# DLRM tower on one core: the first two one-hot fields taken as a couple, a third place for half grams, and another order of tile 3's rows and the dense parts

## What is computed

```python
e = jnp.stack([tbl_0[ids[:, 0]], ..., tbl_25[ids[:, 25]]], axis=1)
T = jnp.concatenate([r_dense[:, None, :], e], axis=1)
Z = jnp.einsum('bnd,bmd->bnm', T, T)
z = Z[:, iu0, iu1]                      # pairs n < m
h = jnp.concatenate([z, r_dense], axis=1)
h = jnp.maximum(h @ W_top1 + b_top1, 0.0)   # 479 -> 512
h = jnp.maximum(h @ W_top2 + b_top2, 0.0)   # 512 -> 256
y = h @ W_top3                              # 256 -> 1
```

## Time and profile before

| what | value |
|---|---|
| times of the kernel before | 118.52, 598.5, 118.72 us; median 118.72 |
| profiled execution | 118.53 us, its span 116.7 us |
| TensorE busy (matmuls, 1008) | 108.4 us, 93% of the span |
| VectorE busy | 85.6 us, 73% |
| ScalarE busy | 80.9 us, 69% |
| GpSimd busy | 65.3 us, 56% |
| one-hot matmuls, lines 473 and 475 | 128 each, 51.8 and 50.2 us busy |
| gram matmuls, line 431 | 512, 15.1 us busy |

### The profile page before, as it was taken

The page is one execution under the profiler, slowest core; times in us unless marked ns, Lnnn a source line. Parts: engine busy times, 40 slices in busy tenths (PEclk is TensorE's granted clock), DMA queues, the critical chain, the costliest instruction groups (busy, mean ns, idle before and its releaser), DMA issues.

```text
span 116.7 us, 2626 instructions
## 1 busy us (share of the span) xinstructions
PE 108.4 (93%) x1008; PEld 91.0 (78%) x1008; DVE 85.6 (73%) x179; ACT 80.9 (69%) x151; POOL 65.3 (56%) x66
## 2 busy tenths in 40 slices
PE   4889799899999999999999999989699998998993
PEld 4757478588688887887888788978599987898990
DVE  5699999889597789969778751499996841567131
ACT  4469990994999999999997794499993602455011
POOL 7387787788777877877787775003063720004000
PEclk9999999999999999999999999999999999999999
DMA  3799749999999529992111112001011110001000
GB/s 74 262 361 406 275 105 411 382 398 363 400 316 380 218 71 367 405 338 65 45 45 32 35 45 60 13 0 26 6 23 51 34 32 6 0 3 21 6 3 1
DMA packets 7751, 17.75 MB, mean 152 GB/s; under 512 B 2078, under 2 KB 3002, under 8 KB 7610
## 3 DMA queue, kind: packets, MB, share of 16 engines
q1 hardware_dynamic: 5770, 14.13, 33.1%
q0 software_dynamic: 1824, 3.25, 9.7%
q10 hardware_dynamic: 144, 0.20, 0.6%
HBM read 17.33 MB, written 0.00 MB: 148 GB/s over the span
## 4 chain that ended last, share of the span: by engine, by line
PE 66%; ACT 11%; DMA 8%; DVE 8%; issue 4%; SPq 1%; ACTq 0%; DVEq 0%
PE work L473 20%; PE work L475 19%; DMA table<-small 8%; PE work L431 8%; PE work L421 6%; PE work L532 5%; ACT Zt L574 4%; PE tp L457 4%; DVE hot L739 3%; PE work L415 3%; ACT t_hi L594 2%; ACT table L566 2%; DVE Zt L574 2%; ACT hot L623 2%; DVE t_lo L708 2%
## 5 line engine op out<-in xcount | busy, mean ns | idle before, releaser
L403 POOL DMA_INDIRECT rows<-tbl,idx x48 | 58.4, 1217 | 18.3 <-issue 13.3
L473 PE MATMUL work<-hot,t_hi 128*128 128x512 f32 x128 | 51.8, 405 | 2.2 <-DVE hot L739 1.1
L475 PE MATMUL work<-hot,t_lo 128*128 128x512 f32 x128 | 50.2, 392 | 0.0
L739 DVE TENSOR_SCALAR hot<-ids_bc,rownum 128x1024 fp32r<-128x1024 int32 (+1 forms) x59 | 38.9, 699 | 7.2 <-PE work L475 7.1
L473 PEld LDWEIGHTS work<-hot,t_hi 128*128 128x128 f32 x128 | 24.0, 188 | 10.8 <-DVE hot L739 2.9
L475 PEld LDWEIGHTS work<-hot,t_lo 128*128 128x128 f32 x128 | 24.1, 188 | 4.4
L594 ACT CAST t_hi<-table 128x1280 fp32r<-128x1280 f32 (+3 forms) x16 | 16.8, 1050 | 5.8 <-DMA table<-small 5.5
L708 DVE TENSOR_TENSOR t_lo<-table,t_hi 128x1280 fp32r<-128x1280 f32 (+3 forms) x16 | 19.5, 1217 | 1.2 <-ACT t_hi L594 1.0
L431 PE MATMUL work<-XT 128*58 128x52 f32 x512 | 15.1, 217 | 2.4 <-ACT Zt L574 1.1
L431 PEld LDWEIGHTS work<-XT 128*58 128x58 f32 x512 | 14.3, 133 | 3.7 <-issue 2.4
L328 POOL DMA_DIRECT2D Zt<-table x9 | 4.7, 531 | 22.1 <-DVE table L566 22.1
(11 more groups left out here) (47 smaller groups left out, 58.1 us busy)
## 6 DMA issues: line engine op xcount, KB each, us to landing
table<-small SPq DMA_DIRECT2D x8, 640.0 KB, 7.9
ids_bc<-ids_oh SPq DMA_DIRECT2D x6, 512.0 KB, 6.1
table<-small SPq DMA_DIRECT2D x4, 512.0 KB, 7.6
w_sb<-w SPq DMA_DIRECT2D x1, 1024.0 KB, 7.7
rows<-tbl,idx POOLq DMA_INDIRECT x48, 4.1
table<-small SPq DMA_DIRECT2D x2, 320.0 KB, 5.0
ids_bc<-ids_oh SPq DMA_DIRECT2D x2, 256.0 KB, 4.5
w_sb<-w SPq DMA_DIRECT2D x1, 512.0 KB, 8.8
```

What stands on the lines that cost most here:

```text
L403: nc.gpsimd.indirect_dma_start(rows[:, t, place - FIRST, :], None, tbls[f], bass.IndirectOffsetOnAxis(ap=idx[:, t, place - FIRST:place - F ...
L473: nc.tensor.matmul(bank, t_hi[:, i % PARTS, c * D:(c + 1) * D], hot[:, k % HOTS, :], start=row_chunk(i, c) == 0, stop=False)
L475: last = nc.tensor.matmul(bank, t_lo[:, i % PARTS, c * D:(c + 1) * D], hot[:, k % HOTS, :], start=False, stop=row_chunk(i, c) == n - 1)
L739: nc.vector.tensor_scalar(hot[:, k % HOTS:k % HOTS + n, :], ids_bc[:, ids_slot(f):ids_slot(f) + n, :], rownum[:, v, at:at + 1], None, ALU. ...
```

## The change

- `SINGLES` goes: fields 0 and 1 are a couple like the others. Only the first chunk of each (`LONE` = 2 chunks) has a one-hot of its own, of width 512; their ids come as two loads, those of field 1 now second in SyncE's queue. ScalarE makes the last couple of chunks of tables 0 and 1.
- Only table 0 comes in parts, of four and four chunks (`HEADED` = 1, `HEAD` = 4, before two tables in three and five); table 1 comes whole. `LOW_PARTS` and ScalarE's first steps follow.
- Ids go to slot f % 6, and the wait for a free slot begins with field 6.
- All eight PSUM banks are one tensor, and `HOMES` gives the place of each half: 0 and 1 as before, and the two `tp` banks for the third half (`IN_TP`). A half waits for the drain of the last half in its own place. The third half waits for the row copies before it; rows (3,1) and (3,2) wait until the third half is drained.
- In the order of steps, rows (3,0) go right behind the look-ups (copied by VectorE), (3,1) behind layer 1 of tile 0 (copied by ScalarE); the dense part of tile 0 goes behind the fourth half, that of tile 2 ahead of the seventh.
- VectorE makes `h1` of tile 2 ahead of its last high copy of the eighth half instead of behind it.

```diff
-VECTOR_ROWS = [(3, 1)]
+VECTOR_ROWS = [(3, 0)]
-HEADED = 2
-HEAD = 3
+HEADED = 1
+HEAD = 4
-SINGLES = 2
+LONE = 2
-ACT_EVERY = 5
-ACT_TABLES = [3, 5, 6, 7, 8, 9, 10, 11, 12, 13]
+ACT_TABLES = [0, 1, 3, 5, 6, 7, 8, 9, 10, 11, 12, 13]
+BANKS = 8
+IN_TP = 3
+HOMES = [0, 1, IN_TP, 0, 1, 0, 1, 0]
-LOW_PARTS = {(i, 5 if i < SINGLES else 4 if OH_CHUNKS[i] == 8 else 6): (i + 1, 0, OH_CHUNKS[i + 1])
-             for i in range(1, K_OH - 1)}
-LOW_PARTS.update({(0, 0): (0, 0, HEAD), (0, 4): (0, HEAD, OH_CHUNKS[0]), (0, 5): (1, 0, HEAD),
-                  (1, 1): (1, HEAD, OH_CHUNKS[1])})
+LOW_PARTS = {(i, 4 if OH_CHUNKS[i] == 8 else 6): (i + 1, 0, OH_CHUNKS[i + 1]) for i in range(K_OH - 1)}
+LOW_PARTS.update({(0, 0): (0, 0, HEAD), (0, HEAD): (0, HEAD, OH_CHUNKS[0]), (0, 6): (1, 0, OH_CHUNKS[1])})
...
-    steps += [("dense", 0, 0), ("burst", 0, 0), ("gram", 0, 0), ("burst", 0, 1), ("gram", 0, 1), ("rows", 3, 0),
-              ("burst", 1, 0), ("gram", 1, 0), ("rows", 3, 1), ("burst", 1, 1), ("gram", 1, 1), ("burst", 2, 0),
-              ("gram", 2, 0), ("layer1", 0, 0), ("layer1", 0, 1), ("burst", 2, 1), ("gram", 2, 1), ("dense", 1, 0),
-              ("layer2", 0, 0), ("layer1", 1, 0), ("layer1", 1, 1), ("rows", 3, 2), ("burst", 3, 0), ("gram", 3, 0),
-              ("dense", 2, 0), ("layer2", 1, 0), ("burst", 3, 1), ("gram", 3, 1), ("layer1", 2, 0), ("layer1", 2, 1),
+    steps += [("rows", 3, 0), ("burst", 0, 0), ("gram", 0, 0), ("burst", 0, 1), ("gram", 0, 1), ("burst", 1, 0),
+              ("gram", 1, 0), ("burst", 1, 1), ("gram", 1, 1), ("dense", 0, 0), ("burst", 2, 0), ("gram", 2, 0),
+              ("layer1", 0, 0), ("layer1", 0, 1), ("rows", 3, 1), ("burst", 2, 1), ("gram", 2, 1), ("dense", 1, 0),
+              ("layer2", 0, 0), ("layer1", 1, 0), ("layer1", 1, 1), ("rows", 3, 2), ("dense", 2, 0), ("burst", 3, 0),
+              ("gram", 3, 0), ("layer2", 1, 0), ("burst", 3, 1), ("gram", 3, 1), ("layer1", 2, 0), ("layer1", 2, 1),
...
+def halves_before(n):
+
+    return max([m + 1 for m in range(n) if HOMES[m] == HOMES[n]], default=0)
...
 def ids_slot(f):

-    return f if f < SINGLES else (f - SINGLES + IDS - 2) % IDS
+    return f % IDS
...
-                n = 1 if i < SINGLES else 2
-                if i >= SINGLES + 2:
-                    sp.wait_ge(hot_used, groups_used(first_hot(ids_free(i))))
-                sp.dma_start(ids_bc[:, ids_slot(i):ids_slot(i) + n, :],
-                             ids_oh[i:i + n, :, :].rearrange("f p b -> p f b")).then_inc(ids_in[i], 16)
+                if i >= IDS:
+                    sp.wait_ge(hot_used, groups_used(first_hot(i - IDS + 2)))
+                sp.dma_start(ids_bc[:, ids_slot(i):ids_slot(i) + 2, :],
+                             ids_oh[i:i + 2, :, :].rearrange("f p b -> p f b")).then_inc(ids_in[i], 16)
...
-            table_ids(0)
+            for f in range(LONE):
+                sp.dma_start(ids_bc[:, f, :], ids_oh[f, :, :]).then_inc(ids_in[f], 16)
...
+                    if IN_TP in HOMES[:halves]:
+                        pe.wait_ge(gram_dve, HOMES.index(IN_TP) + 1)
+                        pe.wait_ge(gram_act, HOMES.index(IN_TP) + 1)
...
-                    if halves >= HALVES:
-                        pe.wait_ge(gram_dve, halves - HALVES + 1)
-                        pe.wait_ge(gram_act, halves - HALVES + 1)
-                    couples(t, i, halves % HALVES, 0, QH // 2).then_inc(burst_done, 1)
+                    if HOMES[halves] == IN_TP:
+                        rows_moved(banks)
+                    if halves_before(halves):
+                        pe.wait_ge(gram_dve, halves_before(halves))
+                        pe.wait_ge(gram_act, halves_before(halves))
+                    couples(t, i, HOMES[halves], 0, QH // 2).then_inc(burst_done, 1)
...
             high_part(0, 0, HEAD)
             distance(0)
             high_part(0, HEAD, OH_CHUNKS[0])
-            one_hot(mine_in(0)[0])
-            high_part(1, 0, HEAD)
-            distance(1)
-            high_part(1, HEAD, OH_CHUNKS[1])
+            high_part(1, 0, OH_CHUNKS[1])
             for kind, t, i in STEPS:
                 if kind == "onehot":
-                    rest = mine_in(i)[1:]
-                    if rest and i < HEADED:
-                        one_hot(rest[0])
-                    if i + 1 < SINGLES:
-                        one_hot(mine_in(i + 1)[0])
-                    if i + 2 < K_OH:
+                    if 1 < i < K_OH - 2:
                         high_part(i + 2, 0, OH_CHUNKS[i + 2])
-                    if i >= SINGLES:
-                        for m in mine_in(i):
-                            one_hot(m)
-                    if 0 < i <= SINGLES:
-                        copy_lookups(i - 1)
-                    elif i > SINGLES + 1:
+                    for m in mine_in(i):
+                        one_hot(m)
+                        if i == 0:
+                            distance(1)
+                    if i <= 1:
+                        high_part(i + 2, 0, OH_CHUNKS[i + 2])
+                    if i > 1:
                         copy_lookups(i - 2)
...
+            def units_done(t):
+
+                if t >= 2:
+                    dve.wait_ge(l2_full, t - 1)
+                dve.wait_ge(l1_part, 2 * (t + 1))
+                nc.vector.tensor_scalar(h1[:, t % 2, :, :], l1[:], 0.0, None, ALU.max).then_inc(h1_ready, 1)
...
-                    copy_high(nc.vector.tensor_copy, t, i, halves % HALVES, first)
+                    copy_high(nc.vector.tensor_copy, t, i, HOMES[halves], first)
+                    if t == TILES - 1 and i == 1:
+                        units_done(t - 1)
                     if t < TILES - 1 or i == 1:
-                        copy_high(nc.vector.tensor_copy, t, i, halves % HALVES, second).then_inc(gram_dve, 1)
+                        copy_high(nc.vector.tensor_copy, t, i, HOMES[halves], second).then_inc(gram_dve, 1)
```

More of the change, by code:

```diff
@@ L265, in dlrm_tower @@
         h1 = apart[:, :, 0:H1].rearrange("p t (u b) -> p t u b", b=P)
-        tp = pb("tp", [P, 2, BATCH])
-        work = pb("work", [P, LOOKUP_BANKS, BANK])
-        gr = work[:, 0:GRAM_BANKS, :].rearrange("p (h k) (q n) -> p h (k q) n", h=HALVES, n=COUPLE * PAD)
+        banks_all = pb("banks_all", [P, BANKS, BANK])
+        tp = banks_all[:, LOOKUP_BANKS:BANKS, :]
+        work = banks_all[:, 0:LOOKUP_BANKS, :]
+        gr = banks_all.rearrange("p (h k) (q n) -> p h (k q) n", k=HALVES, n=COUPLE * PAD)
         l2 = work[:, GRAM_BANKS, :]
@@ L307, in l1_block @@
                 return tp[:, u, 0:P]
-            return work[:, u - COUPLE, 0:P]
+            return work[:, u, 0:P]
         def l2_block(t, v):
@@ L313, in l2_block @@
                 return l2[:, 0:H2] if t < TILES - 2 else work[:, GRAM_BANKS + 1, 0:H2]
-            return work[:, GRAM_BANKS - 1 - v, 0:P]
+            return work[:, 1 - v, 0:P]
         l3 = tp[0:1, 0, P:2 * P]
@@ L607, in distance @@
                 act.wait_ge(ids_in[f], 16)
+                if f == 0:
+                    act.wait_ge(ids_in[1], 16)
                 act.wait_ge(rownum_ready, 2)
@@ L671, in _ @@
                     first, second = range(SAMPLES - ACT_SAMPLES, SAMPLES)
-                    copy_low(nc.scalar.copy, t, i, halves % HALVES, first)
-                    copy_low(nc.scalar.copy, t, i, halves % HALVES, second).then_inc(low_act, 1)
+                    copy_low(nc.scalar.copy, t, i, HOMES[halves], first)
+                    copy_low(nc.scalar.copy, t, i, HOMES[halves], second).then_inc(low_act, 1)
                     if t == TILES - 1 and i == 1:
-                        copy_high(nc.scalar.copy, t, 0, (halves - 1) % HALVES, second).then_inc(gram_act, 1)
-                    copy_high(nc.scalar.copy, t, i, halves % HALVES, first)
+                        copy_high(nc.scalar.copy, t, 0, HOMES[halves - 1], second).then_inc(gram_act, 1)
+                    copy_high(nc.scalar.copy, t, i, HOMES[halves], first)
                     if t < TILES - 1 or i == 1:
-                        copy_high(nc.scalar.copy, t, i, halves % HALVES, second).then_inc(gram_act, 1)
+                        copy_high(nc.scalar.copy, t, i, HOMES[halves], second).then_inc(gram_act, 1)
                     halves += 1
@@ L729, in _ @@
                     dve.wait_ge(ids_in[f], 16)
-                    n = 1 if i < SINGLES else 2
-                    for c in range(0, OH_CHUNKS[i], n):
+                    for c in range(OH_CHUNKS[i]):
                         if (i, c) in LOW_PARTS and i + c:
@@ L833 @@
     for i, n in enumerate(OH_CHUNKS):
-        if i < SINGLES:
-            table = chunks[i]
-        else:
-            f = pair_of(i)
-            part = slice((i - f) * n // 2, (i - f + 1) * n // 2)
-            table = np.stack([chunks[f][:, part], chunks[f + 1][:, part]], axis=2)
+        f = pair_of(i)
+        part = slice((i - f) * n // 2, (i - f + 1) * n // 2)
+        table = np.stack([chunks[f][:, part], chunks[f + 1][:, part]], axis=2)
```

49 lines of the change are left out of this document (23 added, 26 removed).

## The result

| | before | changed kernel |
|---|---|---|
| median | 119.12 us (118.3 to 598.5, 20 runs) | 118.05 us (117.05 to 118.94, 20 runs) |
| ratio to before | | 0.991, 95% interval 0.989 to 0.994 |
| profiled execution, span | 118.53, 116.7 us | 118.94, 117.1 us |

The change takes 1.1 us off. Over 20 runs the kernel before is at 119.12, so 0.4 of the distance from 116.3 to 118.05 is the starting point and the rest a gain of 1.1 in place of 2.4. A ratio here compares only runs within 1.5% of the fastest of their kernel, while a median is over all runs.

What follows compares the result with a forecast made beforehand. It took TensorE to bound the look-ups, with time lost to stops in the start and tail. Profiled 118.53 - 2.5 (tail) + 0.2 (front) = 116.2, or 116.3 us against the median of 118.72; range 115.1 to 117.8.

Steps and rivals of the forecast that it cites:

- The couple makes chunk 16 1.3 us later: Start: wider distance, cast and one-hot in ScalarE's chain move chunk 16 from 15.21 to 16.5, 1.3 us later.
- The 1.1 us of stops behind it go: Chunk 16 to first transposes: ids 4 and 5 with own slots let table 5 come early, removing 1.1 us of stops.
- What is late next: nothing until chunk 46: Look-ups after the start: no new wait until chunk 46, which waits about 0.3 us for ScalarE as before.
- the front's sum: Start up to the first transposes: +1.3 - 1.1 = +0.2 us, with bounds of -0.6 and +1.8.
- Tail -2.5: End of look-ups to layer 1 of tile 3: stops of 3.1 us become 0.6, so it starts at 107.0, not 109.53.
- the low moves of tile 0, issued until 81.7 and 0.4 earlier in the new order (layer 1 asks for them at 83.3): Tail, before layer 1 of tile 0: a cover with no room, costing its own lateness, 0.5 us at most.
- Start ahead: Rival, start: table 1 lands by 7.9, chunk 16 at 15.8, front -0.5, time 115.6 us; chance 0.14.
- Table 1 at 10.2: Rival, start: table 1 lands 7.6 us after issue, the chain moves 1.6 us, time 117.9 us; chance 0.12.
- The third place only moves the wait: Rival, tail: drains become the bound, at 2.75 us each dense 1 waits 1 us, time 117.3 us; chance 0.17.
- Slower by a late table: Rival, start: each microsecond table 1 lands after 8.55 costs one; slower from 13.4, time 121.2 us; chance 0.04.

Runs made afterwards that it cites:

- the new start alone: Kernel before with only fields 0 and 1 as a couple, the id slots and the matching SyncE, ScalarE and VectorE orders, old tail: 1.010 to before.
- the trace with freed slots: Kernel before with only ids of field f in slot f mod 6, so ids 4 and 5 load at once: 1.014 to before.
- the repeated run: The changed kernel timed and traced once more with no edit: 0.993 to before.
- the three traces named under the table: Clock fell to 0.50 for 3 to 4 us: changed, held to chunk 15 (0.995); changed, tables 0 and 1 pairs on VectorE (0.997); slots freed, new tail (0.994).

## Why the prediction was off, step by step

**"The couple makes chunk 16 1.3 us later": right.** It comes at 16.81 in the profiled run (forecast 16.5). By the table's start column, single fields with freed slots have their first transposes at 26.76 (mean of six), the couple at 27.80 (mean of seven, without the two rows at a lower clock in the start): +1.0.

**"The 1.1 us of stops behind it go": right as far as it went.** Single fields with the queue as before or held to chunk 15 have 28.00 (mean of five), with the freed one 26.76: -1.2. The sum of both, -0.2 for the start (forecast +0.2), is the same within the scatter of single traces, 27.4 to 28.8 for one and the same start.

**"What is late next: nothing until chunk 46": this step failed, and with it the front's sum.** It took the look-ups from 27.4 on to last as long as before, since they need the same matmuls, and this is what the earlier trace rows seemed to say: 44.86 busy of 44.97 us. The same number of matmuls took 44.7 to 45.2 us (mean 44.97) in the six traces in which the early loads wait as in before, and 44.7 to 45.0 in four of fourteen with freed slots. In the other ten it was 45.7 to 48.4. The mean over the eight with the couple is 45.59, so +0.6 us; over the six with single fields it is 46.63, so +1.7 (one of them at the lower clock for a while). The full busy share was a share with the slack of the helpers still there, not a promise. The forecast start was +0.2; start and look-ups together measured about -0.2 + 0.6 = +0.4 in the traces with the couple, and +1.1 [0.6, 1.7] in the times of the new start alone. With the tail's 1.1 the sum of the traces is -0.7, where the times say -1.1: single traces do not fix the parts closer than that.

What makes these stops is **not shown**. Shown is that on the start of before they come with the slots being free at once and go with one wait for chunk 15 (1.014 against 0.999), that none of the six traces in which the loads wait that long has them, that in the ten ScalarE or VectorE stands idle 1.3 to 3.0 us at a stretch between 30 and 60 us, where neither is ever idle for 1 us in before, and that the place moves from run to run of one kernel. The instruction queue has a packet about 1.6 us ahead of the late ScalarE copy in the trace with freed slots, and one 0.8 us ahead of the one at 49.43 here, but the stop at chunk 48 in the repeated run has none near it, and before has such packets without stops. That engines wait for their code behind the loads is a suspicion that no run here tested.

**"Tail -2.5": right in order, mis-sized by the wait for the moves.** Every named stop of the earlier trace rows went, four halves run in a row, and dense 2 waits 0.35 us (forecast 0.4). From the end of the look-ups to layer 1 of tile 3 the forecast had 34.7 us (107.0 - 72.33) and the changed kernel took 36.4: 1.7 more, 1.47 of them the stop before layer 1 of tile 0. The failed term is "the low moves of tile 0, issued until 81.7 and 0.4 earlier in the new order (layer 1 asks for them at 83.3)", which was given 0.5 us at most. Rows of the queues in the changed kernel, SyncE and then GpSimd:

```profile
79.86 1.79 SPq L327 DMA_DIRECT2D Zt<-table  x2
81.70 1.20 SPq L363 DMA_DIRECT2D Zt<-table  x2
```

```profile
80.32 1.10 POOL L327 DMA_DIRECT2D Zt<-table  x2 [9.62 <-DVE table L570]
```

On the clock of before (the look-ups end 1.2 us later here) the last move is issued until 81.7, not earlier: 82.90 - 1.2. Layer 1 asks at 85.94 - 1.47 - 1.2 = 83.3, as forecast. What was left out is the time from issue to landing: it starts 3.0 us after the last issue is over. In before it started 3.7 us after it (85.41 - 81.71), and nothing showed. A margin was read as a zero: what the wait needed was 3.0 us, and the new order left it 1.6. With 1.4 taken from 2.5, the 1.1 of the traces is there. The Trainium skill ("DMA: Bandwidth & Descriptors", "Anatomy of one DMA — SWDGE (gpsimd) path") puts some 2 us of fixed cost on a transfer that GpSimd issues, however small, most of it ahead of the completion signal. With its figure, taken for SyncE's moves too, the stop would have been 0.4 as an estimate (81.7 + 2.0 - 83.3). The traces agree in kind, with 3.0 in the changed kernel and at most 2.3 with three moves on GpSimd.

**The rivals.** *Start ahead*: no, the cast of table 1 stood 1.23 us for its DMA until 8.90. *Table 1 at 10.2*: no. *The third place only moves the wait*: half right. Behind the wait for the moves stands the one for `h1`, and no drain was longer than 2.54. *Slower by a late table*: no; the changed start alone is slower than before, but its table 1 comes no later than forecast (the cast starts at 8.16), and its one trace does not show by what.

The clock had no part in the two profiles compared: the earlier trace rows and both windows after have the granted clock at 1.00, in spite of the stop at chunk 12. It can have one in others, as the three traces named under the table show.

**The better version** keeps the tail and leaves the start alone. Its three timings, 0.983, 0.989 and 0.988 (with three moves on GpSimd), are below the changed kernel's 0.991 and 0.993, though not each by more than the intervals. Freed slots held until chunk 7 may add to it (0.977), but the repetition (0.988, and by the median of all runs no gain) leaves that open.

## What to carry to other kernels

For each transfer that a moved step now asks for sooner, write down when its last issue ends and how long before the consumer that was: a wait that shows nothing today is a margin of unknown size, and the landing time behind the issue belongs into the sum. A load that is let go earlier need not be free because its buffer is: test the slot and the moment separately, with a wait that holds the load. And cut every trace at the same marks, since parts of a microsecond show by stretch where medians only say "about the same"; but take several traces, for one and the same start came out between 27.4 and 28.8 us.

## What was not expected of the hardware

In one trace ScalarE stood 2.72 us and VectorE 1.78 us in the middle of a stream whose inputs were long there. Look-ups lengthened by 0.7 us or more came in ten of fourteen traces with early loads and in none of six without; the places moved between runs of one kernel. Small moves within SBUF were used 3.0 us after the end of the last issue (3.2 with four of them on GpSimd: 86.18 - 82.96), but 2.3 with three on each queue, which also issued them sooner than four and two. And the same TensorE stop of 0.75 to 0.96 us for nothing named appeared at 88 to 89 us in both traces in which that wait was gone.
